# Last half of a routed expert layer: rows weighted by diagonal score matrices on TensorE

## The reference, cut to what matters

```python
for e in range(NUM_EXPERTS):
    m = (sorted_ids == e)[:, None]
    out_rows = out_rows + jnp.where(m, h, 0) @ expert_down[e]
out = jnp.zeros_like(hs).at[token_slots].add(out_rows * scores_sorted[:, None])
...
t = t + _L1_ffn_ref(_ln_t(t), ...)
x = _from_tokens(t, x)
```

## Time and profile before

| | us |
|---|---|
| median of three runs (lowest, highest) | 1184.3 (1183.5, 1186.58) |
| the profiled execution's own time | 1183.99 |
| its span, first to last instruction | 1182.2 |
| mean granted TensorE clock over the span | 0.936 of full |

### The profile page before, as it was taken

The page is one execution under the profiler, slowest core; times in us unless marked ns, Lnnn a source line. Parts: engine busy times, 40 slices in busy tenths (PEclk is TensorE's granted clock), DMA queues, the critical chain, the costliest instruction groups (busy, mean ns, idle before and its releaser), DMA issues. The chain is left out here.

```text
span 1182.2 us, 18262 instructions
## 1 busy us (share of the span) xinstructions
PE 1040.3 (88%) x5916; PEld 874.7 (74%) x5916; DVE 713.6 (60%) x1411; ACT 476.2 (40%) x987; POOL 427.2 (36%) x446
## 2 busy tenths in 40 slices
PE   6877787889889997789979999799969999999986
PEld 3555687879888697689977677567857888888864
DVE  5776757986656468768675433765557334444327
ACT  3372236423234245226504335633642344443333
POOL 1105627863762115212212332622431443433421
PEclk9976789999999999999989999999978999999995
DMA  8426738776796366355744547542761689996578
GB/s 275 163 68 245 255 105 278 260 247 236 251 349 244 117 219 243 135 185 210 268 181 158 180 175 267 188 160 91 285 240 45 223 327 335 354 336 210 184 254 306
DMA packets 94664, 261.61 MB, mean 221 GB/s; under 512 B 10041, under 2 KB 48409, under 8 KB 78705
## 3 DMA queue, kind: packets, MB, share of 16 engines
q1 hardware_dynamic: 59800, 173.78, 41.2%
q0 software_dynamic: 14624, 48.64, 11.7%
q10 hardware_dynamic: 20152, 38.02, 10.2%
HBM read 168.59 MB, written 91.82 MB: 220 GB/s over the span
## 5 line engine op out<-in xcount | busy, mean ns | idle before, releaser
L655 POOL TENSOR_TENSOR sb_ring<-sb_raw,sb_ring 128x256 fp32r<-128x256 f32 x192 | 172.7, 931 | 191.0 <-ACT sb_ring L1223 163.2
L716 PE MATMUL ps<-sb_xnH,sb_ring 128*128 128x288 f32 x512 | 163.7, 320 | 18.8 <-DVE sb_sg L1799 7.2
L679 POOL DMA_INDIRECT y_dram<-sb_ysb,sb_target x86 | 86.2, 1003 | 246.2 <-ACT sb_ysb L1308 229.3
L1009 PE MATMUL ps<-sb_w,sb_xtH 128*128 x344 | 153.1, 445 | 13.4 <-DVE sb_hh L1851 11.5
L717 PE MATMUL ps<-sb_xnH,sb_ring 128*128 128x288 f32 x512 | 155.4, 304 | 0.0
L718 PE MATMUL ps<-sb_xnL,sb_ring 128*128 128x288 f32 x512 | 154.8, 302 | 0.0
L1844 DVE TENSOR_TENSOR sb_xtL<-ps,sb_xtH 128x512 fp32r<-128x512 f32 x86 | 59.3, 690 | 144.2 <-ACT sb_xtH L1288 144.1
L1011 PE MATMUL ps<-sb_w,sb_xtH 128*128 x344 | 138.1, 401 | 0.0
L1010 PE MATMUL ps<-sb_w,sb_xtL 128*128 x344 | 137.9, 401 | 0.0
L716 PEld LDWEIGHTS ps<-sb_xnH,sb_ring 128*128 128x128 f32 x512 | 100.5, 196 | 24.5 <-issue 8.5
L670 POOL DMA_INDIRECT sb_xs<-xn_dram,sb_source x86 | 88.1, 1024 | 51.7 <-DVE sb_source L1755 26.5
(11 more groups left out here) (246 smaller groups left out, 2304.1 us busy)
## 6 DMA issues: line engine op xcount, KB each, us to landing
w_dram<-sb_ring SPq DMA_DIRECT2D x48, 1024.0 KB, 5.1
sb_w<-w_dram SPq DMA_DIRECT2D x48, 1024.0 KB, 7.3
sb_ring<-w_dram SPq DMA_DIRECT2D x24, 1024.0 KB, 6.8
sb_raw<-in_w_ffn SPq DMA_DIRECT2D x24, 512.0 KB, 5.9
sb_raw<-in_w_ffn SPq DMA_DIRECT2D x48, 256.0 KB, 5.0
sb_X<-in_x SPq DMA_DIRECT2D x16, 576.0 KB, 8.8
sb_g<-y_dram ACTq DMA_DIRECT2D x18, 512.0 KB, 7.4
xn_dram<-sb_XN ACTq DMA_DIRECT2D x14, 512.0 KB, 5.1
```

Of the source, the lines that this page charges most:

```text
L655: last = pool.tensor_tensor(to[:, 1, cut], raw[:, i % RING, 1, cut], to[:, 0, cut].bitcast(f32), ALU.subtract)
L679: pool.indirect_dma_start(y_dram[h], bass.IndirectOffsetOnAxis(ap=target[:, h, m:m + 1], axis=0), ysb[:, r, :], None).then_inc(y_stored[r] ...
L716: pe.matmul(out_ap, w[0], xh, start=start, stop=False)
L1009: pe.matmul(PS[:, 1, :], xtH[:, i % 2, k, :], wh, start=k == 0, stop=False)
```

## The change

For the second half alone, the two score multiplications leave ScalarE's and VectorE's row passes and go into TensorE's matmuls. ScalarE makes, for each tile, two 128x128 diagonal matrices from the identity `ident`, one scaled by the low scores and one by the high scores (`diag`, a ring of eight tiles, in the memory of `gs` and `gt`). TensorE then multiplies rows by diagonals instead of transposing weighted rows: rows (tokens x 128 channels) as the stationary operand and a diagonal (tokens x tokens) as the moving one give 128 channels x 128 tokens, weighted and transposed. Low and high rows add up in the same PSUM bank. VectorE keeps only the addition into `X`. The low products run three tiles ahead of the high ones. The high rows get a ring of eight places: the four in `g12` and the four in `xs`, which held the gathered rows of the experts.

```diff
+DIAGS = 16 * P // (2 * P)
+HRING = GRING + XSR
...
+        diag = sb("diag", [P, DIAGS, 2, P], f32, comb)
...
+        def high_rows(t):
+            r = t % HRING
+            return g12[:, r, 1, :] if r < GRING else xs[:, r - GRING, :]
...
             for t in range(TL):
                 n = TL + t
-                if t >= GRING:
-                    sp.wait_ge(gt_ready, n - GRING + 1)
-                sp.dma_start(g12[:, n % GRING, 1, :], rows[1, :, t, :]).then_inc(g_loaded[n % GRING], 16)
+                if t == GRING:
+                    sp.wait_ge(t_ready, 2 * NM)
+                if t >= HRING:
+                    sp.wait_ge(f_ready, n - HRING + 1)
+                sp.dma_start(high_rows(t), rows[1, :, t, :]).then_inc(high_loaded(t)[0], 16)
...
+            def add_low(t):
+                n = TL + t
+                if t == 0:
+                    pe.wait_ge(held_loaded, 16 * (HELD // 4 + 2))
+                pe.wait_ge(gs_ready, n + 1)
+                pe.wait_ge(f_added, n - 3)
+                for k in range(KC):
+                    pe.matmul(PS[:, 4 + n % 4, k * P:(k + 1) * P], low_rows(t)[:, k * P:(k + 1) * P],
+                              diag[:, t % DIAGS, 0, :], start=k == 0, stop=False)
+
+            def add_high(t):
+                n = TL + t
+                pe.wait_ge(*high_loaded(t))
+                for k in range(KC):
+                    last = pe.matmul(PS[:, 4 + n % 4, k * P:(k + 1) * P], high_rows(t)[:, k * P:(k + 1) * P],
+                                     diag[:, t % DIAGS, 1, :], start=False, stop=k == KC - 1)
+                last.then_inc(f_ready, 1)
...
-            Beside(combine(1, 0)).finish()
+            for t in range(3):
+                add_low(t)
+            for t in range(TL):
+                add_high(t)
+                if t + 3 < TL:
+                    add_low(t + 3)
...
                     if h:
...
+                        act.wait_ge(f_ready, max(TL, n - DIAGS + 1))
+                        act.activation(diag[:, t % DIAGS, 0, :], ident, ACT.Copy, scale=score[:, h, 0, t:t + 1])
+                        act.activation(diag[:, t % DIAGS, 1, :], ident, ACT.Copy, scale=score[:, h, 1, t:t + 1])\
+                            .then_inc(gs_ready, 1)
+                        continue
...
-            Beside(combine(1, 0)).finish()
+            for t in range(TL):
+                n = TL + t
+                v.wait_ge(f_ready, n + 1)
+                dst = X[:, :, tile_of(1, t)]
+                v.tensor_tensor(dst, dst, PS[:, 4 + n % 4, :].rearrange("p (k n) -> p k n", n=P), ALU.add)\
+                    .then_inc(f_added, 1)
```

More of the change, by code:

```diff
@@ L224, in metaformer @@
         g12 = sb("g12", [P, GRING, 2, CH], f32, comb)
-        gs = sb("gs", [P, 2, CH], f32, comb)
-        gt = sb("gt", [P, 2, CH], f32, comb)
+        weighted_rows = ExitStack()
+        gs = sb("gs", [P, 2, CH], f32, weighted_rows)
+        gt = sb("gt", [P, 2, CH], f32, weighted_rows)
+        weighted_rows.close()
+        diag = sb("diag", [P, DIAGS, 2, P], f32, comb)
         held_too = sb("held_too", [P, TL - HELD - GRING, CH], f32, comb)
@@ L396, in y_stores, with low_rows, high_loaded @@
             return 16 * (((h + 1) * NM - r + 1) // 2)
+        def low_rows(t):
+            if t < HELD:
+                return held[:, t, :]
+            return g12[:, t - HELD, 0, :] if t < HELD + GRING else held_too[:, t - HELD - GRING, :]
+        def high_rows(t):
+            r = t % HRING
+            return g12[:, r, 1, :] if r < GRING else xs[:, r - GRING, :]
+        def high_loaded(t):
+            r, times = t % HRING, t // HRING + 1
+            if r < GRING:
+                return g_loaded[(TL + r) % GRING], 16 * (len(range((TL + r) % GRING, TL, GRING)) + times)
+            parts = sum(16 if q is None else 32 for _, q, _, k in splits if k % RING == r - GRING)
+            return raw_loaded[r - GRING], parts + 16 * times
         def stores(i):
@@ L1333, in combine @@
                     if h:
[L1334 to L1339, removed]
+                        act.wait_ge(f_ready, max(TL, n - DIAGS + 1))
[3 more added lines that the diff above has]
+                        continue
+                    act.wait_ge(g_loaded[n % GRING], 16 * (n // GRING + 1))
                     if n >= 2:
                         act.wait_ge(gt_ready, n - 1)
-                    act.activation(gs[:, n % 2, :], low, ACT.Copy, scale=score[:, h, 0, t:t + 1])\
+                    act.activation(gs[:, n % 2, :], g12[:, n % GRING, 0, :], ACT.Copy, scale=score[:, h, 0, t:t + 1])\
                         .then_inc(gs_ready, 1)
@@ L1863, in combine @@
                         v.wait_ge(gs_ready, n + 1)
-                        if h:
-                            v.wait_ge(g_loaded[n % GRING], 16 * (n // GRING + 1))
                         if n >= 2:
```

## The result

The changed kernel takes 1191.31 us (median of seven runs, 1188.18 to 1194.68); the kernel before, on the same chip, 1184.3 us (1183.24 to 1186.9). The ratio is 1.0064, with a 95% interval of 1.0045 to 1.0083: 5.3 to 9.8 us slower. In a second pair of measurements it was 1.0046 (1.0028 to 1.0064), 3.3 to 7.6 us. The forecast was 1189.7 us and slower, with a range of 1187.5 to 1194.5. The time lies in the range and the direction was right.

A forecast was written before the change was run, and what follows sets the result against it. VectorE was taken as the tail's bound, then TensorE: start 1151.4, 288 records to 1183.1, run-out 0.17, addition 0.7, to 1184.0, +5.9 against 1178.1. Less 0.5 for the store, +5.4 on 1184.3 gives 1189.7 us, range 1187.5 to 1194.5.

The forecast's parts named there:

- VectorE bounds the tail before: In the end stage before the change, VectorE sets the pace at 1.47 us a tile, 25.6 us of work in 26.4.
- Two records for each float32 product: On TensorE in the tail, the 144 added float32 matmuls go through the array twice each, making 288 records.
- 0.110 us a record: TensorE's price per float32 record of 128 columns, ends 0.104 and 0.116; 288 records make 31.7 us.
- ScalarE's pair 0.66 us, TensorE's start: ScalarE makes a tile's two diagonals in 0.66 us; the first pair lets TensorE start at 1151.4.
- Loads at nothing: SyncE's 18 high-row loads in the tail cost nothing; the ring of eight gives 12 us against at most 6.1.
- PSUM at nothing: Low products waiting for an earlier tile's addition to free its bank cost TensorE nothing, with 1 us to spare.
- The clock at 1.00: TensorE's granted clock stays at 1.00 throughout the tail, because it idles less beforehand and then works without a break.
- The end, 3.6 us: The stretch from the last addition to the end of the span, 4.1 us before, becomes 3.6 (3.2 to 4.1).
- one-record: Rival: each diagonal product goes through TensorE once, 15.8 us, and DMA bounds the tail; 1176 or 1178 us, chance 0.04.
- passing fall: Rival: TensorE's clock falls near 1153.9 and comes back, losing 1.7 to 3.3 us; 1191.4 to 1193 us, chance 0.12.
- lasting fall: Rival: TensorE's clock falls in the tail and stays down, 61.9 us for 288 records; 1220 us, chance 0.04.
- Late loads: Rival: eight loads in flight share full DMA engines and TensorE runs dry once, 5 us at most; 1194.7 us, chance 0.05.

The follow-up runs named there:

- the ring alone: The kernel before with only the high rows' ring of eight buffers, weighting left on ScalarE and VectorE; 1180.16 us, ratio 0.9974 to the kernel before.
- the run with 432 records: The changed kernel with every low product issued twice; 1207.51 us, ratio 1.0201 to the kernel before.
- no low products: The changed kernel without its 72 low products, so X gets only the high expert's rows; 1182.06 us, ratio 0.9982 to the kernel before.
- the float32r run: The changed kernel with rows and diagonals of all 144 products read as float32r; 1186.25 us over twelve runs, ratio 1.0002 to the kernel before.
- float32r again: The changed kernel with rows and diagonals read as float32r, run once more for a second profile; 1178.15 us in a single run.

## Why the prediction was right

- **VectorE bounds the tail before.** Right as the bound, wrong in size: 1.47 us a tile was put down to VectorE, of which 1.26 are VectorE's own and the rest waits. The step that failed is adding the mean durations of instructions that overlap by 0.08 us each. So late loads cost more than the text read off the chain: it called the one at 1162.62 mostly covered, and the ring alone took 2.3 us of waits away. Neither enters the sum, because the end after was built from TensorE's records alone.
- **Two records for each float32 product.** Right: 144 calls are 288 records, and the run with one record a call takes the loss away. This step decided the sign.
- **0.110 us a record.** 0.1117: eight every 0.893 us. The term is 288 x 0.1117 = 32.2 us for 31.7, so 0.5 us short, inside its ends. Scaling from 136 columns down to 128, which gave the low end of 0.104, does not hold: 128 columns take 0.1117 us and 136 took 0.111.
- **ScalarE's pair 0.66 us, TensorE's start.** The rows in order of time (start us, us, instruction):

```profile
1153.43 0.60 ACT L1357 ACTIVATE sb_ysb<-ps 128x512 f32<-128x512 f32 x1 [1.99 <-PE ps L1057]
1153.93 0.39 ACT L1384 ACTIVATE sb_diag<-sb_mats,sb_score 128x128 f32<-128x128 f32 x1
1154.22 0.39 ACT L1385 ACTIVATE sb_diag<-sb_mats,sb_score 128x128 f32<-128x128 f32 x1
1154.51 0.39 ACT L1384 ACTIVATE sb_diag<-sb_mats,sb_score 128x128 f32<-128x128 f32 x1
```

  The single copy lasts 0.39 us, as read off the line between the two known shapes; a pair comes every 0.58. TensorE starts 1.28 us after the last copy to `ysb`; 1.2 was the forecast.
- **Loads at nothing.** Right, no instruction of TensorE waited for one. They landed after 2.7 to 7.3 us (median 3.8), in the second profile after up to 7.9, more than the 6.1 that the text had but inside the 12 us that a ring of eight gives. What the text did not see is that the ring alone is worth 0.9 to 1.5 us of tail to the old weighting; in the changed kernel TensorE's records leave nothing of that gain.
- **PSUM at nothing.** Right: TensorE has no idle time inside the stage.
- **The clock at 1.00.** Right in both profiles of the changed kernel and in the run with 432 records. Of the two reasons given, the shorter idle time agrees better with the runs than the unbroken work. TensorE idled 1.31 us ahead of its first product there, and in one of the six profiles with that idle time the clock fell while TensorE ran on, the first with float32r. It idled 2.16 to 2.73 us in the other four (the kernel before twice, the ring alone, no low products), and in all four the clock fell within 1.5 us of TensorE's start. So holding 1.00 was likely, and in part luck.
- **The end, 3.6 us.** 1191.5 - 1187.83 = 3.7.
- **The sum, +5.4 us.** The tail grew by 6.1 and 6.6 us in two pairs of profiles; the medians by 7.0 and 5.6.

Of the rivals, the *one-record* case was the one that decided, and the float32r run shows that it was priced 2 us too low: its tail of 28.1 us is 3.9 below before, where 6 were given. The failed term is the finish after the last load, about 1 us in the text; in the trace it is 1.13 + 0.69 us and some 5 us more to the end of the span, in which the last store lands. A *passing fall* and a *lasting fall* of the clock both exist in this tail; the passing one came without low products, the lasting one with float32r, and neither in the changed kernel's profiles. *Late loads* did not come. The estimate worked out from the Trainium skill's page "Perfetto Trace Analysis", section Engine Utilization, was 107 ns for a 128x128 product; the runs agree for one record (0.1117 us), and a plain float32 product is two of them, 0.223 us.

## What to carry to other kernels

Before moving elementwise weighting to TensorE as products by diagonals, count records, not calls: a float32 product here is two records where a transpose is one, so two weighted rows cost 16 records of 0.11 us against the 4 of a transposed sum, and these 1.79 us a tile are more than the 1.26 that VectorE had needed for the whole tile. Read the pace of an engine from start to start, since mean durations overlap and their sum overstates the work. And try the by-product of a change alone: here the deeper ring of loads, which only accompanied the change, was the part that paid: 1.1 to 5.1 us, of which 0.9 to 1.5 show in the tail.

## What the runs showed of the hardware

- A float32r record and a float32 record of 128 columns take the same 0.112 us at a clock of 1.00 and the float32r one 0.213 at 0.50; the price of float32 is the second record.
- The granted clock may fall in the middle of an unbroken run of TensorE. With float32r products it did at 1159.9, and stayed at 0.50 for the 28 us to the last product; in the same kernel's other profile it held 1.00 through the same stretch. With float32 products it held 1.00 through the 32 us of both profiles of the changed kernel and the 48 us with the low products twice, each begun after TensorE had idled 1.31 us; without low products, begun after 2.73 us, it fell at 1155.0, in an unbroken run that had begun at 1154.9, and came back at 1158.4. An unbroken run is thus no proof against a fall, which the prediction had taken it for.
- In the changed kernel a load of 256 KB lands 2.7 to 7.9 us after its issue (medians 3.8 and 4.2 in its two profiles, with a DMA share of 0.84 in the first between 1160 and 1170). Where TensorE has half the records and the clock held or came back (no low products, float32r again), the median is 5.0 and the last load takes 8.5 and 8.9 us, with DMA engines that are full. A faster engine thus met longer loads.
